# Edges of a group in chunk-major order for TensorE: a graph network on one core

## The reference, cut to what matters

```python
rbf = jnp.exp(coeff * (edge_attr[:, None] - offsets[None, :]) ** 2)   # 32 radial functions
for i in range(DEPTH):                                                # DEPTH = 5
    W = ssp(rbf @ fw1[i] + fb1[i]) @ fw2[i] + fb2[i]                  # ssp: softplus - log 2
    W = W * C[:, None]
    h = x @ lin1_w[i]
    msg = h[src] * W
    agg = jax.ops.segment_sum(msg, dst, num_segments=n) / denom
    x = x + ssp(agg) @ lin2_w[i] + lin2_b[i]
    ...                                                               # layer norm
```

## Time and profile before

| What | Value |
|---|---|
| Median of three runs | 4837.55 us |
| Profiled execution, from its first to its last instruction | 5693.3 us |
| TensorE matmuls busy in it | 2983.2 us (52%) |
| TensorE weight loads busy | 2545.7 us (45%) |
| VectorE busy | 2280.1 us (40%) |
| ScalarE busy | 1229.1 us (22%) |
| GpSimd busy | 3406.5 us (60%) |
| Granted TensorE clock, mean | 0.678 of 2.4 GHz |

### The profile page before, as it was taken

How to read it: one execution, slowest core, us unless ns; L and a number is a source line. 1 busy time by engine, 2 the same in 40 slices (tenths; PEclk the granted TensorE clock), 3 DMA queues, 4 the chain that set the end, 5 groups by cost and what they waited for, 6 DMA issues and landing times. The chain is left out here.

```text
span 5693.3 us, 50135 instructions
## 1 busy us (share of the span) xinstructions
PE 2983.2 (52%) x13205; PEld 2545.7 (45%) x13205; DVE 2280.1 (40%) x4223; ACT 1229.1 (22%) x1929; POOL 3406.5 (60%) x3365
## 2 busy tenths in 40 slices
PE   2333456666466664767647666556665333323323
PEld 2333445555455553555535555445554323223323
DVE  3111344445544455445454444644446233331111
ACT  2000123222233232323323322222223100010000
POOL 5666466564656555656646656456563677746665
PEclk6555578777777786778767877777777555555555
DMA  6111111110111111111111111111110211111111
GB/s 130 45 45 45 40 40 43 40 41 26 45 40 43 40 37 37 44 38 40 44 34 42 41 40 41 30 41 41 38 41 18 54 48 46 47 44 44 47 44 51
DMA packets 167754, 246.56 MB, mean 43 GB/s; under 512 B 77310, under 2 KB 112232, under 8 KB 167708
## 3 DMA queue, kind: packets, MB, share of 16 engines
q0 software_dynamic: 106496, 219.17, 13.6%
q10 hardware_dynamic: 31190, 21.56, 1.5%
q1 hardware_dynamic: 30022, 5.36, 0.5%
HBM read 231.12 MB, written 14.76 MB: 43 GB/s over the span
## 5 line engine op out<-in xcount | busy, mean ns | idle before, releaser
L528 POOL DMA_INDIRECT rows<-table,staged_src x3328 | 3329.3, 1000 | 1999.6 <-issue 1026.8
L626 PE MATMUL pC<-scatter,work 128*128 128x80 f32 x4160 | 710.7, 342 | 1159.0 <-PEq L624 662.3
L626 PEld LDWEIGHTS pC<-scatter,work 128*128 128x128 f32 x4160 | 670.8, 253 | 1375.0 <-issue 1375.0
L595 PE MATMUL pC<-scatter,rows 128*128 128x80 f32 x2496 | 582.5, 419 | 1052.4 <-PEq L589 508.7
L611 PEld LDWEIGHTS pB<-fw,work 128*128 128x128 f32 x4160 | 1035.6, 327 | 199.2 <-issue 177.4
L611 PE MATMUL pB<-fw,work 128*128 (+1 forms) x4160 | 1043.6, 406 | 25.4 <-issue 13.2
L595 PEld LDWEIGHTS pC<-scatter,rows 128*128 128x128 f32 x2496 | 554.4, 329 | 1073.4 <-issue 1073.4
L799 ACT ACTIVATE work<-pA,fb_l 128x512 f32<-128x512 f32 x520 | 356.3, 685 | 2327.7 <-ACTq L859 2276.3
L1072 DVE TENSOR_TENSOR work<-pB,fb 128x512 f32<-128x512 f32 x520 | 354.9, 690 | 1182.2 <-DVEq L1071 826.4
L601 PE MATMUL pA<-basis,fw_q 128*128 (+1 forms) x1040 | 649.5, 710 | 123.6 <-PEq L632 118.7
L994 DVE COPY staged_src<-src_i 128x8 int32 (+1 forms) x416 | 74.8, 180 | 1180.8 <-DVEq L992 1018.8
(11 more groups left out here) (205 smaller groups left out, 1253.1 us busy)
## 6 DMA issues: line engine op xcount, KB each, us to landing
rows<-table,staged_src POOLq DMA_INDIRECT x3328
table<-rows ACTq DMA_DIRECT2D x21, 384.0 KB, 3.1
basis<-in_edge_weight_dram ACTq DMA_DIRECT2D x3, 1664.0 KB
table<-rows ACTq DMA_DIRECT2D x7, 256.0 KB, 2.3
basis<-in_edge_weight_dram ACTq DMA_DIRECT2D x1, 1536.0 KB
table<-rows ACTq DMA_DIRECT2D x7, 192.0 KB, 2.1
table<-rows ACTq DMA_DIRECT2D x3, 396.0 KB, 3.2
x<-in_x_dram ACTq DMA_DIRECT2D x3, 384.0 KB, 8.7
```

What stands on the lines that cost most here:

```text
L528: pool.indirect_dma_start(out=rows[:, q, j, 0:width], out_offset=None, in_=tab[:, :], in_offset=bass.IndirectOffsetOnAxis(ap=staged_src[:, ...
L595: mm = pe.matmul(sum_ps[q % 2], rows[:, q, j, 0:D], scatter[:, q % 2, j, :], start=(j == 0), stop=(j == CH - 1))
L626: mm = pe.matmul(sum_ps[q % 2], msg[:, h, c * D:(c + 1) * D], scatter[:, q % 2, 2 * c + h, :], start=(h == 0 and c == 0), stop=(h == 1 and ...
```

## The change

The edges of a group now lie chunk by chunk for TensorE: column j * 128 + p of a group of `basis` is the edge in partition p, chunk j. To get there, the Square is done group by turn into a scratch tile (`node_work`), and the Exp reads it with a step of 8 elements and writes the turn of `basis` in the new order. Half h is now chunks 4h to 4h + 3. The hidden units read 512 neighbouring columns, the filter of chunk c reads 128 neighbouring columns of `hidden`, and the `msg` product and the sums take the chunks of the new halves.

```diff
                     pe.matmul(pA[:, h * 512:(h + 1) * 512], fw1_q[:, q, :],
-                              basis[:, bass.ds(i * GROUP + h, 512, 2)], start=True, stop=True).then_inc(hid_full[h], 1)
+                              basis[:, bass.ds(i * GROUP + h * 512, 512)], start=True, stop=True).then_inc(hid_full[h], 1)
...
                                 mm = pe.matmul(pB[:, h * 512 + c * D:h * 512 + (c + 1) * D],
-                                               hidden[:, h, c:512:CH // 2], fw2[:, l, :], start=True, stop=True)
+                                               hidden[:, h, c * P:(c + 1) * P], fw2[:, l, :], start=True, stop=True)
...
-                                mm = pe.matmul(sum_ps[q % 2], msg[:, h, c * D:(c + 1) * D], scatter[:, q % 2, 2 * c + h, :],
+                                mm = pe.matmul(sum_ps[q % 2], msg[:, h, c * D:(c + 1) * D], scatter[:, q % 2, h * (CH // 2) + c, :],
...
                     act.wait_ge(basis_w, 16 * (Q + 1))
-                    own(act.activation(basis[:, :], basis[:, :], ACT.Square, bias=neg_offset[:, 0:1]))
                     step = CUTOFF / (RADIAL - 1)
-                    own(act.activation(basis[:, :], basis[:, :], ACT.Exp, scale=-0.5 / (step * step)))
+                    for i in range(TURNS):
+                        turn = basis[:, i * GROUP:(i + 1) * GROUP]
+                        square = node_work[:, (i % 2) * GROUP:(i % 2 + 1) * GROUP]
+                        own(act.activation(square, turn, ACT.Square, bias=neg_offset[:, 0:1]))
+                        own(act.activation(turn.rearrange("p (j e) -> p j e", e=P),
+                                           square.rearrange("p (e j) -> p j e", j=CH),
+                                           ACT.Exp, scale=-0.5 / (step * step)))
...
                             dve.tensor_tensor(msg[:, h, :].rearrange("p (c d) -> p c d", d=D),
                                               filt[:, h, :].rearrange("p (c d) -> p c d", d=D),
-                                              rows[:, q, h:CH:2, 0:D], ALU.mult).then_inc(msg_full[h], 1)
+                                              rows[:, q, h * (CH // 2):(h + 1) * (CH // 2), 0:D], ALU.mult).then_inc(msg_full[h], 1)
```

## The result

Seven runs of the changed kernel took 4847.30 to 4855.71 us, median 4851.08. Seven runs of the kernel before took 4833.23 to 4840.02 us, median 4836.42. The ratio is 1.003, with a 95% interval of 1.0019 to 1.0041: slower by 14.7 us. That is inside the predicted range, on the side of rival 4, and more than the 0.2% (9.7 us) that I took as a difference.

What follows compares the result with a forecast made beforehand. The prediction took GpSimd's gathers to bound the kernel throughout. The terms of the change summed to nothing, so it forecast the median of before, 4838 us, with a range of 4740 to 4890 us.

Steps and rivals of the forecast that it cites:

- rival 4: Gather meetings: groups with late TensorE met less before; TensorE never late costs at most 75 us, 4913 us; chance 0.10.
- Filters: Line 611: neighbouring columns save 2.1 us of TensorE's chain per group, some 556 us in all, nothing on the path.
- Hidden units: Line 601: the read's step goes from 8 bytes to none; taken as nothing, hidden by the gathers.
- basis: Square and Exp: two instructions become 26 and end before ScalarE is next needed; taken as nothing.
- products: Line 1080: same bytes with another step between chunks; taken as nothing, 26 us either way per 0.1 us of the pair.
- Rival 1: TensorE's late chains cause the 0.74 us per group over bare gathers; saves up to 192 us, 4646 us; chance 0.10.
- Rival 3: TensorE stays at 1.2 GHz and a group takes 11.2 us; costs 122 us, 4960 us; chance 0.05.
- Rival 5: Line 611's weights load no faster, it stays near 2.07 us, same time; counted within the 0.60 for no change.
- The terms sum to nothing: All parts of the change together add nothing, so the time stays the median of before, 4838 us.
- the meeting points are fixed: In each convolution group VectorE's instructions hold the third gather 0.14 us and the fifth 0.60 us, together 0.74 us.
- the rebuilt sum of 4840 us: The time before the change, added up from passes and the stretches between them; 0.05% above the median.
- rival 2: Line 1064 slips behind the fifth gather, through a wait on ScalarE's logarithms; 156 us less, 4682 us; chance 0.07.

Runs made afterwards that it cites:

- second profile: The kernel before the change, profiled again with no edit: 4834.52 us.
- after_late: Changed kernel with VectorE's order product 0, softplus 0, product 1, 640-column memset, match, edge factor, softplus 1: 4716.79 us, ratio 0.9787.
- after_between: Changed kernel with VectorE's softplus of the next group's half 0 put between the two products: ratio 0.9834.
- hidden_only: Kernel before with only the basis ordered by halves, so that the hidden units read neighbouring columns: 4839.95 us, ratio 1.0007.

## Why the prediction was right or wrong

**The bound: right.** Gathers bound the kernel, and TensorE's time inside a pass does not enter, as the fourth column of the table shows.

**Filters: right in mechanism, its size too large.** 1.05 us for eight records at full clock, as expected, and 247 ns for a weight load. TensorE saved 316 us, not 556: that sum took the full clock everywhere. At the lower clock (granted 0.50) eight records took 2.13 us before (at 3186.98 in the second profile) and 1.99 after (at 2708.29), a gain of only 0.14 us.

**Hidden units, basis, products: right.** The first alone is 1.0007. Square and Exp take 13 x (1148 + 2063) ns = 41.7 us where two instructions took 22.8, and end at 125.1 us, early in the first pass, which ends near 570. The pair of products is 1.29 us in both.

**Rivals 1, 3 and 5: wrong, as said.** Inside a pass GpSimd is never idle for more than 0.31 us between two gathers, in the changed kernel and in the second profile of before, so it never waits for a buffer there; the granted clock between 620 and 1160 us is 0.81 after and 0.83 before; the weights do load faster.

**The step that failed: "The terms sum to nothing".** It rested on the sentence that the meeting points are fixed, and that on the rebuilt sum of 4840 us, which hit the median. The hit was two errors that cancel. The sum held the gathers of every one of the 260 groups for 0.74 us, 192 us; the second profile of before shows 165.6 us, 118.0 of it, or 0.49 us a group, from the fifth groups on and 47.6 in the first four groups of the passes. The 27 us too many were mostly made good by what the sum had too little of: the first pass took 526.4 us, not 517.9, the gate's 572.1, not 568.3, the last 520.1, not 517.9, and each passage between convolutions 0.5 to 1.1 us more. So before had groups that met less, with room to lose.

**Rival 4 is what happened, by the condition that stood under rival 2.** That rival asked for a wait on ScalarE's logarithms between lines 1080 and 1064, and I looked for it in the changed kernel only. It was there in before: even the profile with the holes has 116 waits of line 1057. "Hidden units that come earlier make this less likely" was right, and it is the mechanism of the loss. The Trainium skill (SBUF — State Buffer, section "Who interferes with whom") says that a VectorE instruction with two SBUF inputs contends with a GpSimd instruction that reads SBUF; the held gathers here agree, and the 640-column memset, the softplus and line 1077 (each of these two with one input in PSUM) held none of the gathers that began beside them (239 in after_late, 258 and 248 in the changed kernel).

**Rival 4's size.** Its bound of 75 us took the 1000 ns of the earlier trace rows, from an execution whose holes had broken up the meetings. With the 0.64 us per group of the second profile, 165.6 / 260, the bound would have been (0.74 - 0.64) x 260 = 26 us. Measured: 178.1 - 165.6 = 12.5 us of held time, of a span longer by 12.8.

## What to carry to other kernels

Where one engine's stream bounds the kernel and another engine can hold it up, a faster third engine moves the meetings and can cost time; lay out the second engine's instructions against the stream, and move them by order or by filler before making anything faster. A rebuilt sum that hits the median doesn't prove its terms: check each against the rows, here the held time per group against the mean of the gathers. And take such a check from an execution whose span agrees with the runs.

## What the runs showed of the hardware

How close a start decides. In after_between, timeline:

```profile
2011.79 0.88 DVE L1069 TENSOR_TENSOR scatter<-onehot,c_e 128x640 f32<-128x640 bf16 x1 [0.22 <-DVEq L927]
2011.82 0.94 POOL L528 DMA_INDIRECT rows<-table,staged_src  x1 [0.30 <-POOLq L526]
```

VectorE began 0.03 us before the gather and did not hold it; it was itself lengthened, from 0.83 to 0.88 us. At 0.10 us it held the gather for 0.61. In all fourteen profiles none of 130 edge-factor products that began up to 0.044 us before a gather held it, and each of 996 that began 0.045 us or more before one did. At that edge the price of a meeting jumps from under 0.08 us, on VectorE, to 0.65 us, on the gather.

A read's step costs TensorE differently in its two roles, in float32. Weights at a step of 16 bytes load in 327 ns instead of 247 over both clocks; the moving operand at 8 bytes is nearly free (712 against 691 ns a record over both clocks) and at 32 bytes nearly doubles at full clock (two records 1.99 us instead of 1.06). The Trainium skill (SBUF — State Buffer, section "Door 1: The DMA port swizzle (why `[64,N]` ≈ `[32,N]`)") gives lines of 16 bytes, with two hits needed per line for the full rate; these three steps agree at full clock. At the lower clock the filters' step costs little, 2.13 against 1.99 us. ScalarE pays as well: the Exp that reads with a step of 32 bytes takes 2063 ns for 1024 columns, the one of hidden_only with a step of 8 bytes 1122, and the Square without a step 1148.
